# Attention scores in a decoder layer: two heads at a time in two halves of TensorE's rows

## The reference: one decoder layer for 32 batches

```python
# self attention with a sparsified softmax
probs = softmax(x @ x.T / 16); mask = probs < 0.01
x = layernorm(x + (normalised probs above 0.01) @ x + 0.01 * (sum below 0.01, broadcast) @ W.T)
# cross attention, 16 heads of width 16, keys and values from the context
q, k, v = split_heads(x @ Wq + bq), split_heads(ctx @ Wk + bk), split_heads(ctx @ Wv + bv)
scores = q @ k.T / 4;  scores = where(mask, -1e15, scores)      # 16 x 112 x 375 a batch
x = layernorm(x + (softmax(scores) @ v) merged @ Wo + bo)
# mixture of experts, 8 experts, the best 2 by softmax
x = layernorm(x + sum of p_e * (x @ Wi[e]) @ Wo[e] over the best two)
```

## Time and profile before

| | |
|---|---|
| median of 3 runs | 868.14 us (867.99 to 869.48) |
| the profiled execution | 868.0 us, span 866.2 us |
| PE busy | 829.0 us, 96% of the span, 7844 matmuls |
| PEld busy | 723.8 us, 84% |
| DVE busy | 723.7 us, 84% |
| ACT busy | 650.5 us, 75% |
| POOL busy | 199.7 us, 23% |
| TensorE's granted clock | 9 tenths or more of full speed in all 40 slices |
| share of PE in the chain that ended last | 87% |

### The profile page before, as it was taken

How to read it: one execution, slowest core, us unless ns; L and a number is a source line. 1 busy time by engine, 2 the same in 40 slices (tenths; PEclk the granted TensorE clock), 3 DMA queues, 4 the chain that set the end, 5 groups by cost and what they waited for, 6 DMA issues and landing times.

```text
span 866.2 us, 25528 instructions
## 1 busy us (share of the span) xinstructions
PE 829.0 (96%) x7844; PEld 723.8 (84%) x7844; DVE 723.7 (84%) x2836; ACT 650.5 (75%) x1961; POOL 199.7 (23%) x293
## 2 busy tenths in 40 slices
PE   4789999999999999999999999999999999999985
PEld 3678888888888888888888888888888888888863
DVE  3547888888998888888988898998888998888765
ACT  2458877788887777888877788887777888777760
POOL 2202122222222222222222212222222222222101
PEclk9999999999999999999999999999999999999999
DMA  8634444443434444433444433444444333433300
GB/s 261 163 98 104 114 108 109 123 114 86 104 98 111 109 115 117 95 98 96 113 109 110 123 94 101 100 106 106 113 118 103 99 100 100 108 86 84 92 8 11
DMA packets 89830, 91.08 MB, mean 105 GB/s; under 512 B 19440, under 2 KB 85600, under 8 KB 89696
## 3 DMA queue, kind: packets, MB, share of 16 engines
q1 hardware_dynamic: 89696, 89.45, 41.0%
HBM read 26.84 MB, written 3.67 MB: 35 GB/s over the span
## 4 chain that ended last, share of the span: by engine, by line
PE 87%; DVE 3%; SPq 3%; DMA 2%; issue 2%; ACT 1%; POOL 1%; DVEq 0%; POOLq 0%; ACTq 0%
PE psum L1042 19%; PE psum L920 18%; PE psum L911 11%; PE psum L936 10%; PE psum L986 8%; PE psum L979 7%; PE psum L968 3%; PE psum L1000 3%; SPq L386 2%; SPq L395 1%; PE psum L957 1%; DVE mix L609 1%; PE psum L950 1%; PE psum L962 1%; DMA wout_sb<-in_wout 1%
## 5 line engine op out<-in xcount | busy, mean ns | idle before, releaser
L475 ACT ACTIVATE probs<-masked,nmax 112x375 f32<-112x375 f32 x512 | 312.9, 611 | 77.6 <-DVE nmax L595 76.6
L595 DVE CUSTOM_DVE_ANT_0 masked<-psum,mask_add 112x375 f32<-112x375 f32 x512 | 276.6, 541 | 53.7 <-PE psum L911 42.8
L505 ACT ACTIVATE probsT<-psum 125x336 f32<-125x336 f32 x512 | 228.6, 447 | 63.2 <-PE psum L920 58.3
L920 PE MATMUL psum<-const_sb,probs 112*125 112x112 f32 x1536 | 251.1, 272 | 0.1
L920 PEld LDWEIGHTS psum<-const_sb,probs 112*125 112x125 f32 x1536 | 235.8, 188 | 16.0 <-issue 6.8
L911 PE MATMUL psum<-k_stack,q_stack 96*112 96x376 f32 x512 | 203.4, 397 | 3.3 <-DMA k_stack<-k_hi 2.7
L418 POOL TENSOR_SCALAR var_eps<-moments 112x1 f32<-112x1 f32 x96 | 21.2, 220 | 485.6 <-DVE moments L699 191.1
L609 DVE SCALAR_TENSOR_TENSOR mix<-psum,gate,mix 112x256 f32<-112x256 f32 x224 | 107.7, 481 | 14.6 <-PE psum L1042 1.3
L1042 PE MATMUL psum<-we_hi,x_hi 128*112 128x512 f32 x256 | 108.0, 422 | 2.4 <-DVE mix L609 2.4
L911 PEld LDWEIGHTS psum<-k_stack,q_stack 96*112 96x112 f32 x512 | 90.1, 176 | 22.5 <-issue 13.4
L1042 PE MATMUL psum<-we_hi,x_lo 128*112 128x512 f32 x256 | 100.8, 394 | 0.0
(11 more groups left out here) (110 smaller groups left out, 1438.2 us busy)
## 6 DMA issues: line engine op xcount, KB each, us to landing
k_stack<-k_hi SPq DMA_DIRECT2D x256, 93.8 KB, 2.2
q_stack<-q_hi SPq DMA_DIRECT2D x256, 56.0 KB, 2.0
ctx_sb<-in_context_T SPq DMA_DIRECT2D x32, 376.0 KB, 3.3
k_stack<-k_lo SPq DMA_DIRECT2D x128, 93.8 KB, 2.2
q_stack<-q_lo SPq DMA_DIRECT2D x128, 56.0 KB, 2.0
xT<-in_x_T SPq DMA_DIRECT2D x32, 112.0 KB, 2.2
x_sb<-in_x SPq DMA_DIRECT2D x32, 112.0 KB, 2.2
out_dram<-out_sb SPq DMA_DIRECT2D x32, 112.0 KB, 1.9
```

Source lines behind the costliest of these rows:

```text
L475: nc.scalar.activation(probs[:, n % RING, :], masked[:, n % RING, :], ACT.Exp, bias=nmax[:, n:n + 1], scale=-1.0, accum_out=probs_sum[a[1] ...
L505: nc.scalar.activation(probsT[:, i % TRING, :], psum[0:KP, T_BANKS[i % 2], 0:KT * TOK], ACT.Copy).then_inc(probsT_copied, 1)
L595: nc.vector.tensor_tensor_reduce(masked[:, n % RING, :], psum[0:TOK, S_BANKS[n % 2], 0:KEYS], mask_add[k][:, :], 1.0, 3.0e38, ALU.add, ALU ...
L920: mm = nc.tensor.transpose(psum[0:KP, T_BANKS[n % 2], j * TOK:(j + 1) * TOK], probs[:, n % RING, j * KP:(j + 1) * KP], ident[0:TOK, 0:TOK])
```

## The change: pairs of heads in rows 0 to 63 and 64 to 127

The stacks get 128 rows. The parts are now interleaved by rows: row 4i + g holds part g of dimension i of the pair, and every fourth row (g = 3) is zero, written once by POOL at the start. So one head of the pair lies in rows 0 to 63 and the other in rows 64 to 127. Each is scored by its own matmul on 64 rows with its own place in the array (`tile_position`), and the queries need no masking: `q_sb` and `head_masks` go, and ACT writes q_hi itself. The factor -1/4 moves into DVE's masking instruction. The weights' columns are put into HEAD_ORDER ahead of the kernel so that pairs stay together.

The scores of a pair are issued together, on PE in odd slots (and slot 18 for the next batch), once both heads of the previous pair are masked; DVE masks both heads of a pair together in even slots. ACT's query writes now wait for eight scores, and DVE's q_lo reads PSUM.

```diff
-        q_sb = sb("q_sb", [128, DC, TOK])
-        q_hi = sb("q_hi", [128, DC, 2, TOK], f32r)
-        q_lo = sb("q_lo", [128, DC, 2, TOK], f32r)
+        q_hi = sb("q_hi", [128, DC, TOK], f32r)
+        q_lo = sb("q_lo", [128, DC, TOK], f32r)
...
-        k_stack = [sb(f"k_stack{k}", [96, DC, PAIRS, KEYS_EVEN], f32r) for k in range(2)]
-        q_stack = [sb(f"q_stack{k}", [96, DC, PAIRS, 2, TOK], f32r) for k in range(2)]
+        k_stack = [sb(f"k_stack{k}", [128, DC, PAIRS, KEYS_EVEN], f32r) for k in range(2)]
+        q_stack = [sb(f"q_stack{k}", [128, DC, PAIRS, TOK], f32r) for k in range(2)]
...
-                 "qT": (act_steps, "q1"), "K0": (dve_steps, "k_lo0"),
+                 "qT": (dve_steps, "q_lo1"), "K0": (dve_steps, "k_lo0"),
...
+                    if it == -1:
+                        sp.wait_ge(setup_pool, 5)
...
-                            sp.dma_start(q_stack[1 - k][32 * g:32 * g + 32, :, n, :, :].bitcast(fp32),
-                                         part[32 * n:32 * n + 32, :, :, :].bitcast(fp32))\
+                            sp.dma_start(q_stack[1 - k][g:128:4, :, n, :].bitcast(fp32),
+                                         part[32 * n:32 * n + 32, :, :].bitcast(fp32))\
...
-                            sp.dma_start(k_stack[1 - k][32 * g:32 * g + 32, :, n, 0:KEYS].bitcast(fp32),
+                            sp.dma_start(k_stack[1 - k][g:128:4, :, n, 0:KEYS].bitcast(fp32),
...
-            pool.wait_ge(setup_pool, 1)
+            for k in range(2):
+                nc.gpsimd.memset(k_stack[k][:, :, :, :].bitcast(fp32), 0.0).then_inc(setup_pool, 1)
+                nc.gpsimd.memset(q_stack[k][:, :, :, :].bitcast(fp32), 0.0).then_inc(setup_pool, 1)
+            pool.wait_ge(setup_pool, 5)
...
-                        BIG, None, ALU.mult).then_inc(pool_proj.did("mask"), 1)
+                        -BIG / Q_SCALE, None, ALU.mult).then_inc(pool_proj.did("mask"), 1)
...
                     if proj and n == 3:
                         act.wait_ge(pe_proj.sem, pe_proj.to("qT", p))
+                        if attn:
+
+                            act.wait_ge(scores_ready, count(a, HEADS, CHUNK_HEADS))
                         for c in range(DC):
                             nc.scalar.activation(
-                                q_sb[:, c, :], bank_of["qT"][:, c * TOK:(c + 1) * TOK], ACT.Identity,
+                                q_hi[:, c, :], bank_of["qT"][:, c * TOK:(c + 1) * TOK], ACT.Identity,
...
-                        mask_add[k][:, :], 1.0, 3.0e38, ALU.add, ALU.min,
+                        mask_add[k][:, :], -Q_SCALE, 3.0e38, ALU.add, ALU.min,
...
+                def low_queries(c):
+                    dve.wait_ge(act_proj.sem, act_proj.to(f"q_hi{DC - 1}", p))
+                    nc.vector.scalar_tensor_tensor(
+                        out=q_lo[:, c, :], in0=bank_of["qT"][:, c * TOK:(c + 1) * TOK], scalar=bq_col[:, c:c + 1],
+                        in1=q_hi[:, c, :].bitcast(fp32), op0=ALU.add, op1=ALU.subtract)\
+                          .then_inc(dve_proj.did(f"q_lo{c}"), 1)
...
-                    if attn and 1 < n < HEADS:
+                    if attn and 1 < n < HEADS and n % 2 == 0:
                         head(a, n)
+                        head(a, n + 1)
...
                     if n == 4 and proj:
-
-                        dve.wait_ge(act_proj.sem, act_proj.to("q1", p))
-                        if attn:
-
-                            dve.wait_ge(scores_ready, count(a, HEADS, PAIRS))
-                        for half in range(2):
-                            nc.vector.tensor_scalar(
-                                q_hi[:, :, half, :], q_sb[:, :, :], head_masks[:, half:half + 1], None, ALU.mult)\
-                                  .then_inc(dve_proj.did(f"q_hi{half}"), 1)
+                        for c in range(DC):
+                            low_queries(c)
...
-                def scores(a, n):
+                def scores(a, pair):
                     k = a[1] % 2
-                    if n < PAIRS:
-                        pe.wait_ge(q_stacked[k][n], turn(a, 3))
-                        pe.wait_ge(k_stacked[k][n], turn(a, 3))
+                    if pair < PAIRS:
+                        pe.wait_ge(q_stacked[k][pair], turn(a, 3))
+                        pe.wait_ge(k_stacked[k][pair], turn(a, 3))
-
-                    if due(count(a, HEADS, n - 1)):
-                        pe.wait_ge(masked_ready, count(a, HEADS, n - 1))
-                    c, pair, odd = HEAD_ORDER[n] // CHUNK_HEADS, HEAD_ORDER[n] % CHUNK_HEADS // 2, HEAD_ORDER[n] % 2
-                    nc.tensor.matmul(psum[0:TOK, S_BANKS[n % 2], 0:KEYS_EVEN], q_stack[k][:, c, pair, odd, :],
-                                     k_stack[k][:, c, pair, :], start=True, stop=True)\
-                                       .then_inc(scores_ready, 1)
+
+                    if due(count(a, HEADS, 2 * pair)):
+                        pe.wait_ge(masked_ready, count(a, HEADS, 2 * pair))
+                    for odd in range(2):
+                        rows = slice(64 * odd, 64 * odd + 64)
+                        nc.tensor.matmul(psum[0:TOK, S_BANKS[odd], 0:KEYS_EVEN],
+                                         q_stack[k][rows, pair // PAIRS, pair % PAIRS, :],
+                                         k_stack[k][rows, pair // PAIRS, pair % PAIRS, :], start=True, stop=True,
+                                         tile_position=(64 * odd, 0)).then_inc(scores_ready, 1)
...
-                    if attn and 0 < n < HEADS - 1:
-                        scores(a, n + 1)
-                    if n >= SLOTS - 2 and active("attn", it + 1):
-                        scores(p, n - (SLOTS - 2))
+                    if attn and n % 2 and n < HEADS - 1:
+                        scores(a, (n + 1) // 2)
+                    if n == SLOTS - 2 and active("attn", it + 1):
+                        scores(p, 0)
```

More of the change, by code:

```diff
@@ L141, in sem @@
             return ctx.enter_context(nc.semaphore(name))
-        const_sb = sb("const_sb", [128, 128 + 2 + EXPERTS])
+        const_sb = sb("const_sb", [128, 128 + EXPERTS])
         ident = const_sb[:, 0:128]
-        head_masks = const_sb[:, 128:130]
-        expert_ids = const_sb[0:TOK, 130:130 + EXPERTS]
+        expert_ids = const_sb[0:TOK, 128:128 + EXPERTS]
         ones = sb("ones", [128, TOK])
@@ L265, in decoder_layer @@
             ("self", ["ctx_hi", "self_exp", "sparseT"]),
-            ("proj", ["x1T", "q0", "q1", "k_hi0", "k_hi1"]),
+            ("proj", ["x1T", "q_hi0", "q_hi1", "k_hi0", "k_hi1"]),
             ("join", ["o_sb", "x2_hi", "gate_exp"]),
@@ L512, in iteration @@
                         act.wait_ge(pe_proj.sem, pe_proj.to("qT", p))
+                        if attn:
+                            act.wait_ge(scores_ready, count(a, HEADS, CHUNK_HEADS))
                         for c in range(DC):
                             nc.scalar.activation(
-                                q_sb[:, c, :], bank_of["qT"][:, c * TOK:(c + 1) * TOK], ACT.Identity,
-                                bias=bq_col[:, c:c + 1]).then_inc(act_proj.did(f"q{c}"), 1)
+                                q_hi[:, c, :], bank_of["qT"][:, c * TOK:(c + 1) * TOK], ACT.Identity,
+                                bias=bq_col[:, c:c + 1]).then_inc(act_proj.did(f"q_hi{c}"), 1)
                     if own and n == 6:
@@ L561, in _ @@
                 nc.vector.memset(v_sb[k][:, :, :, 1, :], 0.0)
-                nc.vector.memset(k_stack[k][:, :, :, KEYS:KEYS_EVEN].bitcast(fp32), 0.0)
             nc.vector.memset(ones[:, :], 1.0).then_inc(setup_dve, 1)
@@ L655, in iteration @@
                     if n == 4 and proj:
-                        dve.wait_ge(act_proj.sem, act_proj.to("q1", p))
-                        if attn:
-                            dve.wait_ge(scores_ready, count(a, HEADS, PAIRS))
-                        for half in range(2):
-                            nc.vector.tensor_scalar(
-                                q_hi[:, :, half, :], q_sb[:, :, :], head_masks[:, half:half + 1], None, ALU.mult)\
-                                  .then_inc(dve_proj.did(f"q_hi{half}"), 1)
-                    if n == 5 and proj:
-                        for half in range(2):
-                            dve.wait_ge(dve_proj.sem, dve_proj.to("q_hi1", p))
-                            nc.vector.scalar_tensor_tensor(
-                                out=q_lo[:, :, half, :], in0=q_sb[:, :, :],
-                                scalar=head_masks[:, half:half + 1],
-                                in1=q_hi[:, :, half, :].bitcast(fp32), op0=ALU.mult, op1=ALU.subtract)\
-                                  .then_inc(dve_proj.did(f"q_lo{half}"), 1)
+                        for c in range(DC):
+                            low_queries(c)
                     if n == 5:
@@ L840, in iteration @@
                             head(p, 0)
+                            head(p, 1)
                         if join:
@@ L864, in iteration @@
```

(13 more changed lines are left out.)

2 lines of the change are left out of this document (1 added, 1 removed).

## The result

The kernel after takes 1016.96 us (median of 4, 1015.64 to 1024.41) against 868.57 us before: 1.1721 times as long, 95% interval 1.1681 to 1.1761. The forecast was 1000 us in a range of 888 to 1030. The profiled execution took 1016.75 us with a span of 1014.9.

The account below looks back on a forecast made before the run. PE, busy 96% of the span and waiting for no other engine, was taken to bound the kernel, so anything added to its stream is paid 32 times. 868 + 64 + 51 + 15 + 2 = 1000 us, range 888 to 1030.

Parts of the forecast that it names:

- Term 1: PE's eight score pairs: 0.64 us each with emptying and exposed loads, net +2.0 us an iteration, 64 us.
- a sign of being wrong: PE's score pairs: the prediction is wrong if the two scores of a pair cost less than 0.4 us together.
- Term 2: Slots 5 and 6: PE stalls 1.65 us for copies behind ACT's q wait, 51 us; T: pair 3's first load starts.
- Term 3: Slot 14: DVE masks heads 14 and 15 before experts 4 and 5, delaying PE's V1 0.5 us, 15 us.
- The sentence that DVE is in time elsewhere: Other pairs: DVE masks both old heads in time; heads 4 and 5 end about a microsecond ahead of slot 5.
- Term 4: Kernel start: POOL zeroes both stacks, 7,808 words a partition, before ctx_lo; 2 us, bounds 0 to 10.
- A: Pairs: halves overlap without emptying the array, a pair costs 0.26 us, ACT's wait stays; 896 us, chance 0.13.
- B: ACT's wait at q is covered, ACT being behind enough that it opens for free; 947 us, chance 0.08.
- C: Pairs: the two halves do not overlap, tiles cost +2.6 us an iteration; 1020 us, chance 0.09.
- D: Overlap pays for itself if a pair costs one plain step (0.17 us) and stalls are small; 835 us, chance 0.07.
- E: Only POOL's start costs; the change does not overlap, empty or stall; 870 us, chance 0.03.

Follow-up runs that it names:

- e7: Kernel after, ACT's q after six scores instead of eight, head 15 masked behind the expert adds, out_sb behind the masks of heads 2 and 3: 914.4 us.
- e6: Kernel before with untiled scores and masks in pair order, head 15 masked behind the expert adds, out_sb behind the masks of heads 2 and 3: 880.3 us.
- e1: Kernel after, PE waiting for the fourth pair's stacks together with the third's, so ACT writes q after six scores, not eight: 931.88 us.
- e3: Kernel before with one added wait, ACT's query writes waiting for seven scores; no tiles, no pairs: 939.73 us.
- e2: e1 with one more edit: DVE adds experts 4 and 5 ahead of head 15's mask: 925.03 us.
- e9: Kernel after with useless matmuls filling PE's two stalls, nine behind the score of slot 5, three ahead of slot 6's transposes: 994.44 us.
- e8: Kernel after with one head a slot, 16 excursions a batch instead of 8, and ACT's wait early at five scores: 1032.42 us.

## Why the prediction was right, point by point

**What bounds the kernel.** Right: whatever made PE wait or lengthened its stream was paid a batch at a time.

**Term 1, the tiles (+64 us forecast).** The mechanism held, the size is too large. Gaps and exposed loads are there on both sides of a pair, as I had priced them. Mis-sized: I gave the second half 0.09 us for its load; loads and streams of both halves run together, so a pair is 0.36 us to the next start and about 0.54 with what is lost on both sides, not 0.64. That alone is 0.8 us a batch too much. Against it stood the way in behind Wo, 0.28 where I had 0.10 for emptying and 0.1 more. The 0.36 is below the 0.4 us that I had named as a sign of being wrong; with what is lost around the pair it is above, and the text of the sign didn't say which of the two it meant. The second half did not start 0.09 behind the first, as I had written, but with it. With order and waits mended, tiled pairs stand 46 us over the kernel before (e7), 18 less than forecast, and 34 over untiled pairs in the same order (e6).

**Term 2, ACT's wait (+51 us).** Right in place, and each step on ACT came within 0.05 us; PE's idle time is 1.21 and 0.45 us, 1.66 together, against 1.65. That agreement hides two errors. PE went on 0.17 us later than I had it, both times, and without the wait it would have gone on sooner than I had it (T + 0.35 in e1, not T + 0.45). From start to start the stall is 1.92 us, 60 us in 31 batches. e3 shows that the wait does it alone.

**Term 3, DVE's order (+15 us).** The place was right and its size nearly (0.44 against 0.5 us), but what mending it gives back is 7 us, not 13 (e2), as the next wait takes half. The sentence that DVE is in time elsewhere failed: in the order of pairs PE also waits in slot 3 for heads 2 and 3, which stand behind out_sb and POOL. Moving out_sb gave 10.6 us in the tiled kernel and 15.9 in the untiled one, there with fewer waits for DMAs. In the kernel after, PE's matmuls wait for masks only once, 0.4 us (100 to 800 us), so this place shows only once the others are mended.

**Term 4, the start (+2 us).** Right to be near nothing: the memsets take 6.9 us for 7,808 words, and a DMA for which POOL waits lands later.

**The sum** came to 1000, 17 us under the measured time, and that it is so close is luck in part, for errors of opposite sign stand in it. Measured are 46 us for the tiled pairs (e7), 60 for the stall (e1 against the kernel after), 22.5 for the clock (e9) and 17.5 for the two places of DVE (e1 to e7), together 146 of the 148 us. So Term 1 was 18 us too large, Term 2 about 9 too small, DVE's part 2 too small, and the clock, 22.5 us, was in no term; the 2 us of Term 4 show nowhere. The step that failed is the one I did not take: I priced a stall of PE at its idle time, and never asked what PE's idling does to the matmuls behind it.

**The rivals.** Of A, the overlap of the halves held, but the emptying that it left out is there, as the gaps around the pair and the price of e8 show. B, ACT's wait covered, did not happen by itself; e1 made it happen: 932, where I had 947. C (no overlap) falls with the equal 0.36 us of a pair and of a lone half. D fails at its first condition, since a pair did not cost one plain step. E falls with the result.

## What to carry to other kernels

Price a change of the array's tiling at the excursion, not at the tile: here it costs about 0.54 us for a pair and as much for a lone half, against 0.17 us for an untiled score whose load is hidden, so two halves that overlap wholly still lose here (0.54 us against 0.34 for two untiled scores with hidden loads). I conclude, without a run that shows it, that a form must be kept for more matmuls before it can pay. When a semaphore's count is raised because work is regrouped (four scores became eight), find the slot in which the new count is reached and list what is queued behind the wait: this one wait was 85 of 148 us, and waiting for the DMAs one pair earlier took it away. A stall of PE costs more than the idle time that the profile shows: measure it from start to start (1.92 us against 1.66 here), and look at the clock behind it (another 22.5 us in all).

## What the runs showed of the hardware that I had not expected

- Two row tiles of 64 rows took 0.43 us together, loads included, and one alone 0.43 (e8); their two loads took 0.17 us, the time of one.
- Stalls of 1.21 and 0.44 us, with some 0.9 us of work between them, were followed by some 3.5 us at 1.2 GHz. Filling them with useless matmuls made the kernel 22.5 us faster (1016.96 to 994.44) and brought the mean granted clock from 0.963 to 0.990.
- Changing the array's form 16 to 32 times a batch did not lower the clock so: 0.993 in e1 with 8 pairs a batch; 0.985 to 0.994 in the four runs of e8 with 16 single excursions, where the kernel before shows 0.986 to 0.994.
- POOL's memset wrote 3,008 words a partition in 2.60 us, 0.86 ns a word, where its subtraction of 752 words took 1.77 us.
